# Two linear attentions run in steps beside an edge pass instead of in stages of their own

## The chip, the cores and the metric

The kernel runs on one core of a Trainium2 chip. The metric is the device time of one execution in microseconds. The kernel before took 8725.7 us (median of 3 runs, 8723.53 to 8730.71).

## The reference, cut to what matters

The program is a network of four layers over N = 3125 nodes with 256 features and 50000 edges sorted by target. Each layer takes the layer norm `xn` of `x` and adds two things to `x`: a graph convolution and an attention over all nodes. A feed-forward block follows. Only layers 1 and 3 matter here:

```python
# layer 1: attention without a softmax over pairs of nodes (4 heads of 32); k is exp'ed over the nodes
x = x + L1_gnn(xn, edge_index, edge_weight) + L1_mix(xn)     # both read xn alone
# L1_gnn, first of two convolutions
h = relu(x @ w1 + b1); agg = segment_sum(ew[:, None] * h[src], dst); h = agg @ w2 + b2
# layer 3: 4 heads of 64; k and v are layer-normed per head
k = _layer_norm(k, ln_k_g, ln_k_b); v = _layer_norm(v, ln_v_g, ln_v_b)
kv = einsum('bhsd,bhse->bhde', k, v) / S;  ga = einsum('bhsd,bhde->bhse', q, kv);  ga @ wo.T + bo
# L3_gnn: three graph convolutions with 1/sqrt(degree) on both sides
h = tanh(conv(x, W1, b1)); h = tanh(conv(h, W2, b2)); out = conv(h, W3, b3)
```

Both linear attentions compute a small matrix from all nodes first (k times v) and multiply every node's q by it afterwards. Neither needs anything of the graph convolution, nor the other way round.

## The kernel before, in words

All engines run one program each, written out by hand in order (`tensor_program`, `scalar_program`, `vector_program`, `gpsimd_program`, `sync_program`). An engine executes its instructions in that order. The stages are cut by `rest`: every engine drains, raises a semaphore and waits until all five have. Nodes lie in 25 tiles of 125 (`T`, `P`); `CH` are 7 chunks of 500 or 375 nodes. SBUF is one tensor, `arena`, cut by hand with `at(offset, ...)`. PSUM is 8 banks given out in turn by `Banks.take`, which also returns the key of the bank's holder before, so that the taker waits until that one was read. `put`, `land` and `of` are semaphores with a key for each value.

An edge pass (`pass_pool`, `pass_pe`, `pass_dve`) sums messages over sorted edges in KC = 416 steps of 128 edges. In step k POOL gathers 128 rows from a table in device memory (L1828), into a ring of `RING` = 6 buffers; it waits until the matmul of step k - 6 is done. DVE builds a one-hot matrix (L1861, with edge weights L1863), into a ring of 4, two steps ahead. PE multiplies the one-hot matrix by the rows (L1843), which the trace records as two matmuls with a weight load each. DVE adds the bank to the target tile (L1881), with a register for the tile's offset. Layer 1 has two such passes (`c1a`, `c1b`, rows of 256), layer 3 has three (`d3a` with 256, `d3c` with 512, `d3e` with 256), and layers 0 and 2 have one each, with attention weights per head: there DVE also multiplies the gathered rows in place (L1871).

The order around the change, before:

- Layer 1: the layer norm `n1`; `rest`; the attention as a stage (`l1_mix_*`, L632 to L749); `rest`; `l1_gnn_*`: SP loads 4 weights, 2 biases and 10 vectors (L2295, L2297, L134), PE waits for all of them and makes the table's rows (L297, L300), DVE and ACT add the bias and apply relu (L2342, L2343, L2356), SP writes the table in 5 DMAs (L2291), and the pass `c1a` begins.
- Layer 3: the norm `n3`; `rest`; the attention (`l3_mix_*`, L574 to L619, with `heads_*` and `queries_*`); `rest`; `l3_gnn_*`: SP loads, DVE scales the rows by the degree (L2537), SP writes the table, and the pass `d3a` begins.

In the attention of layer 3, k and v of a unit of 5 tiles are copied out of PSUM, centred per head, squared, summed and scaled (DVE L359 to L381; ACT L409, L414), then PE sums k times v over all tiles (L441), then for each chunk come q (L459), q times kv (L469), and the output product (L596), which DVE adds to X (L305). The functions that the change touches:

## Time and profile before

| | |
|---|---|
| median of 3 runs | 8725.7 us |
| profiled execution | 8726.65 us, span 8724.9 us |
| PE busy | 6441.2 us, 74% |
| DVE busy | 4647.5 us, 53% |
| POOL busy | 3782.1 us, 43% |
| ACT busy | 1029.3 us, 12% |
| mean granted TensorE clock | 0.736 of 2.4 GHz |

The shares are means over some twenty stages with different limits. The change concerns the two attention stages (77.68 us and 198.31 us) and the two passes behind them (529.7 us and 529.4 us), so those stretches have to be read one by one.

### The profile page before, as it was taken

The page shows a single profiled execution, that of the slowest core. Times are in us where ns is not written, and L with a number is a line of the kernel's source. Part 1 is how long each engine was busy: PE and PEld are TensorE (multiplying, and loading weights), DVE is VectorE, ACT ScalarE, POOL GpSimd, SP SyncE. Part 2 cuts the span into 40 slices and gives each one's busy share as a digit, 9 for nine tenths or more (in the row PEclk, how much of TensorE's full clock was granted, in tenths as well). Part 3 has the DMA queues.
Part 4 walks back from the last instruction along what each step waited for, and adds up shares of the span by engine and source line. Part 5 has one row for each costly group of instructions (what it writes and reads, how often), then busy time and mean ns, then how long its engine had stood idle before and what let it go on. Part 6 is the DMA issues. An engine that isn't in the chain of part 4 may idle for free. (4 is left out here: it accounts for less than half of the span.)

```text
span 8724.9 us, 74385 instructions
## 1 busy us (share of the span) xinstructions
PE 6441.2 (74%) x22206; PEld 3621.3 (42%) x22206; DVE 4647.5 (53%) x11112; ACT 1029.3 (12%) x2395; POOL 3782.1 (43%) x3733
## 2 busy tenths in 40 slices
PE   5756878838688677666769777496788888885786
PEld 4443433326433333355434423264333223433675
DVE  7574467772345455542454577866443586455211
ACT  2211001112100100111220011111001000000121
POOL 1874037705267467334000067300674575673222
PEclk9987556659865666679875576687566999565898
DMA  1101223326233233246001133200332565332554
GB/s 50 41 18 38 94 71 106 105 58 182 73 100 105 62 104 105 56 136 159 8 32 76 46 95 108 58 18 6 111 105 63 163 207 163 102 105 63 166 160 130
DMA packets 335705, 796.30 MB, mean 91 GB/s; under 512 B 79773, under 2 KB 189364, under 8 KB 321146
## 3 DMA queue, kind: packets, MB, share of 16 engines
q0 software_dynamic: 202752, 490.56, 21.3%
q1 hardware_dynamic: 132563, 300.99, 10.2%
q8 instruction: 190, 3.11, 0.1%
q14 instruction: 200, 1.64, 0.1%
HBM read 714.20 MB, written 77.09 MB: 91 GB/s over the span
## 5 line engine op out<-in xcount | busy, mean ns | idle before, releaser
L1843 PE MATMUL bank<-arena 128*125 128x256 f32 (+3 forms) x5824 | 3059.9, 631 | 763.2 <-DMA arena<-TAB,arena 353.5
L1828 POOL DMA_INDIRECT arena<-TAB,arena x2080 | 1967.1, 946 | 1596.7 <-DMA TAB<-arena 957.2
L1843 PEld LDWEIGHTS bank<-arena 128*125 128x125 f32 x5824 | 1248.1, 265 | 2573.6 <-DVE arena L1861 862.9
L1881 DVE TENSOR_TENSOR arena<-bank,arena 125x256 f32 (+3 forms) x2912 | 1359.5, 467 | 1381.0 <-PE bank L1843 1238.2
L1828 POOL DMA_INDIRECT arena<-TABa,arena x832 | 808.3, 972 | 1629.6 <-SPq L138 1374.2
L1861 DVE TENSOR_SCALAR arena<-arena 128x125 f32<-128x125 f32 x2080 | 674.3, 325 | 51.0 <-DMA TAB<-arena 50.9
L1465 POOL DMA_INDIRECT REC<-arena x400 | 471.8, 1180 | 290.1 <-DVE arena L1683 168.4
L1107 PE MATMUL bank<-arena 128*128 128x256 f32 x2048 | 484.9, 393 | 139.0 <-DVE arena L1265 70.7
L1056 POOL DMA_INDIRECT SUM<-arena x192 | 307.7, 1603 | 625.2 <-DVE arena L1277 590.3
L1274 DVE TENSOR_TENSOR arena<-bank,arena 128x512 f32<-128x512 f32 x96 | 66.4, 692 | 925.2 <-PE bank L1121 925.2
L297 PE MATMUL bank<-arena 128*125 128x256 f32 (+2 forms) x1600 | 426.9, 424 | 163.1 <-issue 40.1
L2027 PE MATMUL bank<-arena 125*128 125x100 bf16 (+1 forms) x2496 | 462.8, 321 | 53.3 <-DVE arena L2077 53.0
L1107 PEld LDWEIGHTS bank<-arena 128*128 128x128 f32 x2048 | 393.9, 196 | 214.3 <-issue 159.0
L1121 PE MATMUL bank<-arena 128*128 128x256 f32 x2048 | 458.7, 379 | 0.0
L1041 POOL DMA_INDIRECT arena<-XNT,arena x192 | 210.9, 1098 | 571.3 <-DVE arena L1244 513.7
L297 PEld LDWEIGHTS bank<-arena 128*125 128x125 f32 x1600 | 304.0, 199 | 279.9 <-issue 156.3
L1121 PEld LDWEIGHTS bank<-arena 128*128 128x128 f32 x2048 | 388.0, 189 | 55.6
L262 PE MATMUL bank<-arena 125*128 125x125 f32 x450 | 96.4, 398 | 391.3 <-DVE arena L239 336.4
L1143 ACT ACTIVATE arena<-bank,arena 128x256 f32<-128x256 f32 x512 | 242.9, 474 | 1027.3 <-PE bank L1107 1027.3
L1871 DVE TENSOR_TENSOR arena<-arena 128x260 f32<-128x260 f32 (+1 forms) x832 | 352.7, 424 | 20.2 <-DMA arena<-TABa,arena 19.4
L2077 DVE TENSOR_SCALAR arena<-arena 125x2048 bf16<-125x2048 bf16 x156 | 107.6, 746 | 350.8 <-DMA arena<-STR 350.8
L1863 DVE TENSOR_SCALAR arena<-arena 128x125 f32<-128x125 f32 x832 | 289.5, 349 | 0.0
(459 smaller groups left out, 6016.7 us busy)
## 6 DMA issues: line engine op xcount, KB each, us to landing
arena<-L_ffn_pack SPq DMA_DIRECT2D x32, 2054.0 KB, 8.8
arena<-L_ffn_pack SPq DMA_DIRECT2D x64, 1026.0 KB, 5.7
arena<-TAB,arena POOLq DMA_INDIRECT x2080, 2.8
arena<-SLR SPq DMA_DIRECT2D x52, 500.0 KB
arena<-DLR SPq DMA_DIRECT2D x52, 500.0 KB
arena<-TABa,arena POOLq DMA_INDIRECT x832, 2.8
TAB<-arena SPq DMA_DIRECT2D x20, 625.0 KB
arena<-L_ffn_b SPq DMA_DIRECT2D x96, 128.0 KB, 5.5
```

Source lines behind the costliest of these rows:

```text
L297: ins = e.matmul(ps[0:P, 0:f], srcT[:, kk, t * P:(t + 1) * P], W[:, kk, f0:f0 + f], start=(kk == 0), stop=(kk == k - 1 and not odd))
L1056: e.indirect_dma_start(out=SUM[:, :], out_offset=bass.IndirectOffsetOnAxis(ap=m.ridi[:, 2 * k + j:2 * k + j + 1], axis=0), in_=m.Y[k % 2][ ...
L1107: ins = e.matmul(ps[:, 0:SLOTS], w1[:, kk, oo * 128:(oo + 1) * 128], m.XE[i][:, kk, :], start=(kk == 0), stop=(kk == 1))
L1121: ins = e.matmul(ps[:, j * D:(j + 1) * D], m.H[i][:, kk, j * 128:(j + 1) * 128], w2[:, kk, :], start=(kk == 0), stop=(kk == m.hp - 1))
L1465: e.indirect_dma_start(out=REC[:, :], out_offset=bass.IndirectOffsetOnAxis(ap=ADR[:, b:b + 1], axis=0), in_=VAL[:, b, :], in_offset=None). ...
L1828: e.indirect_dma_start(out=m.G[k % RING][:, 0:m.width], out_offset=None, in_=m.table[:, :], in_offset=bass.IndirectOffsetOnAxis(ap=eidx[:, ...
L1843: e.matmul(ps[0:P, 0:m.full], m.S[k % SRING], m.G[k % RING], start=True, stop=True).then_inc(*put("pass_p", m.g, "summed", k))
L1861: ins = e.tensor_scalar(m.S[k % SRING], iotaL, edl[:, k:k + 1], None, ALU.is_equal)
L1863: ins = e.tensor_scalar(m.S[k % SRING], iotaL, edl[:, k:k + 1], m.weight[:, k:k + 1], ALU.is_equal, ALU.mult)
L1871: e.tensor_tensor(v, v, bcast(m.factor[:, k, :], c, 2), ALU.mult).then_inc(*put("pass_v", m.g, "weighed", k))
L1881: e.tensor_tensor(o, banks.of(m.g, "added", k)[0:P, 0:m.full], o, ALU.add).then_inc(*put("pass_v", m.g, "added", k))
L2027: e.matmul(o, sl[:, k * 128:(k + 1) * 128], a.as3[s], start=(s == 0), stop=False)
```

## The change

The stages of the attentions of layers 1 and 3 are taken out, with one `rest` each, on all five engines. Their PE and DVE programs become generators that yield a step number before each piece of work, and `pass_pe` and `pass_dve` of `c1a` and `d3a` run every piece whose number is due before their own step k. ACT, which has nothing to do in these passes, gets its part as one block in front of its next work. During these two passes the pass uses banks 0 to 3 and the attention banks 4 to 7 (in layer 3 two of them for projections, two for the pair of sums).

```diff
+    def beside(steps):
+        due = [next(steps, None)] if steps else [None]
+        def upto(k):
+            while due[0] is not None and due[0] <= k:
+                due[0] = next(steps, None)
+        return upto
-    def pass_pe(e, m):
+    def pass_pe(e, m, steps=None):
+        upto = beside(steps)
         for k in range(KC):
-            ps, before = banks.take(m.g, "added", k)
+            upto(k)
+            ps, before = banks.take(m.g, "added", k, **(LOW if steps else {}))
...
         for k in range(KC + 1):
+            upto(k)
             onehot(k + 2)
...
     def l3_mix_dve(e):
+        def spread(u):
+            yield U3 * u + 24
+            e.wait_ge(*of(g, "squared", u))
+            e.tensor_reduce(s2, tv, AX, ALU.add)
...
+        def scale(u):
+            yield U3 * u + 29
+            e.wait_ge(*of(g, "std", u))
+            e.reciprocal(s3, s3)
+            yield U3 * u + 30
+            e.tensor_tensor(vv, vv, bcast(s3, 64, 2), ALU.mult)
+            yield U3 * u + 33
+            e.tensor_tensor(vv, vv, bcast(gg, 20), ALU.mult)
+            yield U3 * u + 36
+            e.tensor_tensor(vv, vv, bcast(bb, 20), ALU.add)
...
+    def l3_weights_dve(e):
+        for W in m3W[1:]:
+            v = W.rearrange("p k (h c) -> p (k h) c", c=64)
+            settle(e, e.tensor_reduce(m3mean, v, AX, ALU.add), "mix_v")
+            settle(e, e.tensor_scalar(m3mean, m3mean, 1.0 / 64, None, ALU.mult), "mix_v")
+            settle(e, e.tensor_tensor(v, v, bcast(m3mean, 64, 2), ALU.subtract), "mix_v", "m3", "centred")
+        e.tensor_tensor(X, X, bcast(m3bo, T), ALU.add)
...
     def l3_gnn_sp(e):
+        l3_mix_sp(e)
+        table_sp(e, "d3a", TAB, d3acc, lambda t: ("d3a", "u", t))
         vec_t(e, d3b1, inp["L3_gnn_b1"]).then_inc(*land("deg_w"))
...
-        for v, name in ((d3W1, "W1"), (d3W2, "W2"), (d3W3, "W3")):
-            e.dma_start(v, mat(inp["L3_gnn_" + name])).then_inc(*land("deg_w", "d3", "loads"))
-        table_sp(e, "d3a", TAB, d3acc, lambda t: ("d3a", "u", t))
+        e.dma_start(d3W1, mat(inp["L3_gnn_W1"])).then_inc(*land("deg_w", "d3", "loads"))
+        e.wait_ge(*of("m3", "mm", T - 1))
+        for v, name in ((d3W2, "W2"), (d3W3, "W3")):
+            e.dma_start(v, mat(inp["L3_gnn_" + name])).then_inc(*land("deg_l", "d3", "later"))
...
     def l1_gnn_sp(e):
-        for v, name in zip(c1w, ("c1_w1", "c1_w2", "c2_w1", "c2_w2")):
-            e.dma_start(v, mat(inp["L1_gnn_" + name])).then_inc(*land("conv_w"))
+        e.dma_start(c1w[0], mat(inp["L1_gnn_c1_w1"])).then_inc(*land("conv_f"))
+        e.dma_start(c1bias[0], vec_n("L1_gnn_c1_b1")).then_inc(*land("conv_f", "c1a", "weights"))
+        l1_mix_sp(e)
+        for v, name in zip(c1w[1:], ("c1_w2", "c2_w1", "c2_w2")):
+            e.dma_start(v, mat(inp["L1_gnn_" + name])).then_inc(*land("conv_w"))
...
-        l1_mix_pe(e)
-        r = rest(e, r + 1)
-        banks.clear()
```

In layer 1 the work is the same (all copies out of PSUM now lie on ACT; before every second one was DVE's), the maximum of k is taken chunk by chunk, and the bias is added to X in 5 pieces. In layer 3 the centring of k and v (L359, L361, L363) is gone, replaced by six small operations on the weights in front of the pass (`l3_weights_dve`), and all copies are ACT's. In layer 1, `c1a` waits for its first weight and bias alone.

On PE, at the queries of layer 3, the program before had (L459 is q, L469 is q times kv, L596 the output product, L1843 the pass):

```order
L459 MATMUL bank<-arena 128x500 x4
L469 MATMUL bank<-arena 128x500 x2
L596 MATMUL bank<-arena 125x256 x8
L459 MATMUL bank<-arena 128x375 x4
L469 MATMUL bank<-arena 128x375 x2
L596 MATMUL bank<-arena 125x256 x6
...
L1843 MATMUL bank<-arena 125x256 x416
L1843 MATMUL bank<-arena 125x512 x416
```

Now one chunk of queries stands like this (L1988 is the pass, L643 is q, L653 is q times kv, L664 the output product):

```order
L643 MATMUL bank<-arena 128x500 x2
L1988 MATMUL bank<-arena 125x256
L643 MATMUL bank<-arena 128x500 x2
L1988 MATMUL bank<-arena 125x256 x5
L653 MATMUL bank<-arena 128x500
L1988 MATMUL bank<-arena 125x256
L653 MATMUL bank<-arena 128x500
L1988 MATMUL bank<-arena 125x256 x5
L664 MATMUL bank<-arena 125x256 x2
L1988 MATMUL bank<-arena 125x256 x2
L664 MATMUL bank<-arena 125x256 x2
```

A chunk's work is spread over 19 steps of the pass, at most two matmuls at a place.

On DVE, in the same pass, the program before repeated three rows (L1861 the one-hot, L1881 the add):

```order
L2537 TENSOR_SCALAR arena<-arena 125x256 x25
L1861 TENSOR_SCALAR arena<-arena 128x125 x4
L1875 TENSOR_LOAD arena
L1881 ISA
L1881 TENSOR_TENSOR arena<-bank,arena 125x256
L1861 TENSOR_SCALAR arena<-arena 128x125
```

Now the scaling of a unit of k or v stands between them (L2008 the one-hot, L2028 the add, L732, L735 and L738 the attention):

```order
L732 RECIPROCAL arena<-arena 125x20
L2008 TENSOR_SCALAR arena<-arena 128x125
L2028 ISA
L2028 TENSOR_TENSOR arena<-bank,arena 125x256
L735 TENSOR_TENSOR arena<-arena 125x1280
L2008 TENSOR_SCALAR arena<-arena 128x125
L2028 ISA
L2028 TENSOR_TENSOR arena<-bank,arena 125x256
L2008 TENSOR_SCALAR arena<-arena 128x125
```

Three operations of 125x1280 and one reduction of that size stand in every 24 steps, each alone in front of a one-hot.

On SP, at the start of layer 3's convolution, the program before had (W are the three weight matrices):

```order
L579 DMA arena<-woT 128x2x256
L580 DMA arena<-L_mix_bo 125x256
L134 DMA arena<-L_gnn_b 128x4x1 x2
L2450 DMA arena<-L_gnn_b 125x256
L2452 DMA arena<-L_gnn_W 128x2x512
L2452 DMA arena<-L_gnn_W 128x4x512
L2452 DMA arena<-L_gnn_W 128x4x256
L2291 DMA TAB<-arena 125x5x256 x5
```

Now the attention's 9 loads (the last two are shown) stand right in front of the table:

```order
L609 DMA arena<-woT 128x2x256
L610 DMA arena<-L_mix_bo 125x256
L2440 DMA TAB<-arena 125x5x256 x5
L134 DMA arena<-L_gnn_b 128x4x1 x2
L2607 DMA arena<-L_gnn_b 125x256
L2608 DMA arena<-L_gnn_W 128x2x512
L2611 DMA arena<-L_gnn_W 128x4x512
L2611 DMA arena<-L_gnn_W 128x4x256
```

The convolution's own loads moved behind the table's five writes.

## Rows read from the trace of the kernel before

**Rows 1.** Windows: layer 1's attention, table, pass c1a; layer 3's likewise; passes d3c, a0.
```profile
core 0: us, PE busy (x) PEld busy (x) DVE busy (x) ACT busy (x) POOL busy (x), PEclk, DMA share, GB/s
2308.29:2385.97 77.68, 61.76 (x295) 41.42 (x295) 29.82 (x60) 19.14 (x44) 0.00 (x0) 0.95 0.03 9
2385.97:2439.76 53.79, 33.58 (x124) 22.40 (x124) 16.01 (x31) 4.61 (x12) 5.43 (x2) 0.80 0.28 84
2439.76:2969.50 529.74, 436.34 (x833) 190.87 (x833) 286.54 (x828) 0.00 (x0) 393.58 (x416) 0.60 0.38 103
5907.19:6105.50 198.31, 126.82 (x484) 92.59 (x484) 129.91 (x158) 30.50 (x58) 0.00 (x0) 0.80 0.03 7
6105.50:6145.50 40.00, 0.00 (x0) 0.00 (x0) 7.76 (x30) 0.00 (x0) 0.00 (x0) 0.53 0.41 136
6145.50:6674.90 529.40, 445.39 (x832) 195.32 (x832) 259.33 (x829) 0.00 (x0) 393.40 (x416) 0.58 0.38 104
6839.00:7375.50 536.50, 452.72 (x862) 132.42 (x863) 427.26 (x844) 3.52 (x6) 390.50 (x414) 0.98 0.69 203
1223.00:1805.00 582.00, 444.50 (x832) 183.43 (x832) 445.45 (x1348) 86.46 (x418) 406.57 (x416) 0.61 0.37 96
```

**Rows 2.** Timeline of pass d3a, first steps: start, us, engine, line, operation.
```profile
6145.50 0.96 POOL L1828 DMA_INDIRECT arena<-TAB,arena  x1 [579.64 <-DMA TAB<-arena]
6146.76 0.95 POOL L1828 DMA_INDIRECT arena<-TAB,arena  x1 [0.30 <-issue]
6148.38 11.93 PE L1843 MATMUL bank<-arena 128*125 128x256 f32 x19 [43.42 <-DMA arena<-TAB,arena]
6149.72 0.43 DVE L1881 TENSOR_TENSOR arena<-bank,arena 125x256 f32 x1 [4.07 <-PE bank L1843]
```

**Rows 3.** Timeline, last steps of d3a: one step's matmuls, last gather, last add.
```profile
6661.73 1.19 PE L1843 MATMUL bank<-arena 128*125 128x256 f32 x2 [0.49 <-DMA arena<-TAB,arena]
6665.06 0.94 POOL L1828 DMA_INDIRECT arena<-TAB,arena  x1 [0.93 <-PE bank L1843]
6674.44 0.42 DVE L1881 TENSOR_TENSOR arena<-bank,arena 125x256 f32 x1 [0.90 <-PE bank L1843]
```

**Rows 4.** Timeline of SP, DVE and PE at the starts of both attentions and convolutions.
```profile
2312.95 6.83 DVE L720 TENSOR_TENSOR arena<-arena 125x6400 f32<-125x6400 f32 x1 [5.28 <-DMA arena<-L_mix_b_out]
2385.97 1.92 SPq L2295 DMA_DIRECT2D arena<-L_gnn_c_w  x4
2386.03 5.63 DVE L2411 TENSOR_SCALAR arena<-arena 128x416 int32<-128x416 f32 x1
2397.10 3.75 PE L297 MATMUL bank<-arena 128*125 128x256 f32 x8 [11.67 <-DMA arena<-L_gnn_bn_b]
2406.13 25.68 SPq L2291 DMA_DIRECT2D TAB<-arena  x5
5910.99 0.58 SPq L580 DMA_DIRECT2D arena<-L_mix_bo  x1
5917.30 6.83 DVE L608 TENSOR_TENSOR arena<-arena 125x6400 f32<-125x6400 f32 x1 [10.73 <-DMA arena<-L_mix_bo]
6105.57 0.38 DVE L2535 TENSOR_SCALAR arena<-arena 128x416 int32<-128x416 f32 x1
6109.30 25.31 SPq L2291 DMA_DIRECT2D TAB<-arena  x5
```

**Rows 5.** Groups by form in 5907.19 to 6105.50: DVE work that stays, per operation.
```profile
L377 DVE TENSOR_TENSOR arena<-arena 125x1280 f32<-125x1280 f32 x10 | 14.9, 1493 | 0.3
L305 DVE TENSOR_TENSOR arena<-bank,arena 125x256 f32<-125x256 f32 x25 | 10.6, 424 | 13.4 <-PE bank L596 13.4
```

**Rows 6.** Timeline of POOL in pass a0, 1434 to 1446: the lengthened gathers.
```profile
1437.43 1.23 POOL L1828 DMA_INDIRECT arena<-TABa,arena  x1 [0.30 <-PE bank L1843]
1438.96 1.12 POOL L1828 DMA_INDIRECT arena<-TABa,arena  x1 [0.30 <-PE bank L1843]
```

More of the change, by code:

```diff
@@ L63, in restart @@
     def restart(self):
-        self.n, self.held = 0, [None] * 8
+        self.n, self.held = {}, [None] * 8
     def clear(self):
@@ L286, in norm_pe, with lin_n_pe @@
         turn_pe(e, g, XN, lambda t: (g, "tile", t))
-    def lin_n_pe(e, g, srcT, k, W, f, tiles, f0=0, bias=None, sem="lin_p"):
+    def lin_n_pe(e, g, srcT, k, W, f, tiles, f0=0, bias=None, sem="lin_p", lo=0, hi=8):
         for t in tiles:
-            ps, before = banks.take(g, "out", t)
+            ps, before = banks.take(g, "out", t, lo=lo, hi=hi)
             if before:
@@ L583, in l3_mix_pe @@
         g = "m3"
-        heads_pe(e, g)
-        for ci, (n0, w) in enumerate(CH):
-            i = ci % 2
-            queries_pe(e, g, ci, (g, "kvs", 1))
+        yield 0
+        e.wait_ge(*of(g, "centred"))
+        for u in range(len(UNITS) + 1):
+            if u < len(UNITS):
+                t0, k = UNITS[u]
+                for j in range(5):
+                    yield U3 * u + 4 * j
+                    lin_n_pe(e, g + "kv"[k], XT, 2, m3W[1 + k], D, (t0 + j,), sem="mix_p", **PROJ)
+            if u and u % 2 == 0:
+                if u == 2:
+                    pair = [banks.take(g, "kvs", k, **PAIR)[0] for k in range(2)]
+                for j in range(5):
+                    yield U3 * u + 18 + j
+                    t = 5 * (u // 2 - 1) + j
+                    if j == 0:
+                        e.wait_ge(*of(g, "headed", u - 1))
+                    for k in range(2):
+                        ins = e.matmul(pair[k][:, 0:128], m3kN[:, t, k * 128:(k + 1) * 128],
+                                       m3vN[:, t, k * 128:(k + 1) * 128], start=(t == 0), stop=(t == T - 1))
+                        if t == T - 1:
+                            ins.then_inc(*put("mix_p", g, "kvsum", k))
@@ new lines, in l3_mix_pe @@
+        for ci, (n0, w) in enumerate(CH):
+            c0 = U3 * len(UNITS) + 24 + 19 * ci
+            for oo in range(2):
+                yield c0 + oo
+                ps, before = banks.take(g, "q", ci, oo, **PROJ)
+                if before:
+                    e.wait_ge(*of(*before))
+                for kk in range(2):
+                    ins = e.matmul(ps[:, 0:w], m3W[0][:, kk, oo * 128:(oo + 1) * 128], XT[:, kk, n0:n0 + w],
+                                   start=(kk == 0), stop=(kk == 1))
+                ins.then_inc(*put("mix_p", g, "qmm", ci, oo))
+            for k in range(2):
+                yield c0 + 6 + k
+                e.wait_ge(*of(g, "kvs", k))
+                e.wait_ge(*of(g, "q", ci, k))
+                ps, before = banks.take(g, "r", ci, k, **PAIR)
+                if before:
+                    e.wait_ge(*of(*before))
+                e.matmul(ps[:, 0:w], m3kvs[:, k, :], m3qc[ci % 2][:, k, 0:w], start=True, stop=True).then_inc(
+                    *put("mix_p", g, "rmm", ci, k))
@@ L638, in l1_mix_pe @@
         g = "m1"
-        e.wait_ge(*of(g, "loads"))
         for ci, (n0, w) in enumerate(CH):
-            ps, before = banks.take(g, "kT", ci)
+            yield 8 * ci
+            if ci == 0:
+                e.wait_ge(*of(g, "loads"))
+            ps, before = banks.take(g, "kT", ci, **HIGH)
             if before:
@@ L668, in l1_mix_pe @@
             ins.then_inc(*put("mix_p", g, "qmm", ci))
-            ps, before = banks.take(g, "o", ci)
+            yield c0 + 5
+            ps, before = banks.take(g, "o", ci, **HIGH)
             if before:
@@ L1851, in pass_act, with pass_dve @@
                 *put("pass_s", m.g, "extra", k))
-    def pass_dve(e, m):
+    def pass_dve(e, m, steps=None):
+        upto = beside(steps)
         offs = []
@@ L2308, in l1_gnn_pool, with conv_pe @@
             pass_pool(e, c1pass[g], (g, "table"))
-    def conv_pe(e, g, src, wa, wb, bias, ready=None):
-        e.wait_ge(*of("c1", "loads"))
+    def conv_pe(e, g, src, wa, wb, bias, ready=None, steps=None):
+        e.wait_ge(*of(*(("c1", "loads") if ready else (g, "weights"))))
         if ready:
@@ L2336, in conv_pe, with conv_dve @@
                 ins.then_inc(*put("conv_p", g, "secondmm", ci, oo))
-    def conv_dve(e, g, ba):
-        e.wait_ge(*of("c1", "loads"))
+    def conv_dve(e, g, ba, steps=None):
+        e.wait_ge(*of(*(("c1a", "weights") if steps else ("c1", "loads"))))
         for t in range(0, T, 2):
@@ L2344, in conv_dve @@
         e.wait_ge(*of(g, "zero"))
-        pass_dve(e, c1pass[g])
+        pass_dve(e, c1pass[g], steps)
+        e.wait_ge(*of("c1", "loads"))
         for ci, (n0, w) in enumerate(CH):
```

242 lines of the change are left out of this document (149 added, 93 removed).

## The prediction, made before the changed kernel ran

> **What bounds the kernel now.** I read the windows of the four stretches that the change touches, then the timeline inside the passes, then their ends. The windows [rows 1] say where the two attentions stand: 77.68 us in layer 1 and 198.31 us in layer 3, in which POOL does nothing, PE is busy for 61.76 and 126.82 us and DVE for 29.82 and 129.91 us. Behind each comes a stretch that makes the table (53.79 and 40.00 us) and then a pass of 529.7 and 529.4 us. In the passes PE looks fullest (436.34 and 445.39 us), but the time is POOL's. The first gather of d3a starts at 6145.50, the next 1.26 us later [rows 2], and the last of 416 at 6665.06 [rows 3], so the mean distance is 519.56 / 415 = 1.252 us: 0.95 us of gather and 0.30 us between two. PE needs two matmuls a step, 1.19 us from the first's start to the second's end [rows 3], and they are pipelined. What shows the room is the distance from a gather to the add of the same step: 6149.72 - 6145.50 = 4.2 us [rows 2]. The gather ring has 6 buffers, that is 6 x 1.25 = 7.5 us until POOL would wait. So PE and DVE together may come 3.3 us late before POOL loses anything, and whatever they are late by beyond that is lost for good, since POOL can't catch up. DVE is busy for 259.33 of 529.4 us [rows 1]. The pass d3c shows more: its matmuls have 512 columns, twice as many, PE is busy for 452.72 us, and the pass still takes 536.5 us. The granted clock there is 0.98, in d3a it is 0.58 (of the two levels, mostly the lower, 1.2 GHz).
>
> **Layer 1, what goes.** The attention's stage, from its first load to the next stage's first, is 77.7 us [rows 1]. Then c1a waits for 2 loads instead of 16. Before, PE starts 2397.10 - 2385.97 = 11.1 us after the stage's start [rows 4]. For the short wait the nearest row is the attention's own, where three loads were issued from 2308.29 on and the first work on them starts at 2312.95 [rows 1, 4]: 4.7 us. That gives 6.4 us, if SP isn't late with the table: the first table write follows PE's start by 2406.13 - 2397.10 = 9.0 us, so it can go at 13.7 us, and SP's 19 loads in front of it take about 19 x 0.48 = 9.1 us (four took 1.92 [rows 4]). Ends: 0 (PE's start hidden by DVE, which is held for 5.63 us, or by SP) and 7. I take 6.4.
>
> **Layer 3, what goes.** 198.3 us of stage [rows 1]. SP has 9 loads before the table instead of 6: they took from 5907.19 to 5910.99 + 0.58 = 5911.57, so 4.4 us, against 6109.30 - 6105.50 = 3.8 us [rows 1, 4]: +0.6 us. The attention's loads land at 5917.30, 10.1 us after the stage's start; then DVE does the six operations on the weights and the bias (6.83 us [rows 4]). None of the six is larger than an operation of 1280 elements (1.49 us [rows 5]), so all is done by 10.1 + 9 + 6.8 = 26 us, and the first gather needs 40.0 us for the table's sake [rows 1]. Cost nothing, with 14 us of cover.
>
> **What comes into the passes: PE.** By busy time it doesn't fit at today's clocks: 445.39 + 126.82 = 572 us in a pass of 529.4. At the lower level throughout, with the attention's busy time scaled from its clock of 0.80 to 0.5, it is 126.82 x 1.6 = 203 us, and 445 + 203 - 529 = 119 us too much; in c1a 61.76 x 0.95 / 0.5 = 117 and 436 + 117 - 530 = 24 us. That is one end, 143 us. At the upper level d3c shows twice the columns of d3a in 452.72 us of busy time, so d3a's own work takes about 226 us (an estimate, half of it) and the attention's about 126.82 x 0.80 = 101 us: 327 of 529 us, which fits easily; the other end is 0. Which clock? Columns per step of 1.25 us, from the code: d3a has 512 and gets 0.58, d3c has 1024 and gets 0.98. The attention of layer 3 adds on average 305 (127,100 columns in 416 steps), that of layer 1 167 (69,500). And where the lower level makes PE late, PE is busy without a gap; the attention's stage with such stretches has 0.80. So I expect a clock near 0.85 in d3a, near 0.75 in c1a, with intervals at the lower level in which PE falls behind by some tenths of a microsecond per step, most of it inside the 3.3 us. The nearest row is d3c, which has just that: 536.5 us against 529.4, of which some is its longer add. I take 8 us for d3a and 3 us for c1a.
>
> **DVE and the waits in order.** What stays of layer 3's DVE work is 4 operations of about 1.49 us in each of 10 units, 10.6 us of adds [rows 5] and some 5 us of small ones: 75 us, so 334 of 529. Pass a0 goes at the gathers' rhythm with 445.45 us of DVE [rows 1]. Cost nothing. Every piece of the attention waits in PE's and DVE's order, with the pass behind it. Each needs a copy by ACT, which is idle in both passes (0.00 us [rows 1]), and the numbers in the code leave two steps or more, 2.5 us, except where the second q matmul takes the bank of a product that DVE adds just then; that is under 1 us, 6 times, and inside the 3.3 us. Cost nothing; it is gone if PE is late already.
>
> **POOL's gathers beside long DVE operations.** 30 products of 125x1280 in layer 3 and 5 additions in layer 1, both inputs in SBUF, now run while POOL gathers. Of such company the trace has pass a0, where DVE multiplies the gathered rows: POOL is busy for 406.57 us against 393.40 in d3a [rows 1], with single gathers of 1.23 and 1.12 us [rows 6]. 13.2 us over 416 products is 0.032 us each; by their length, 1.49 to 0.42, it is 0.11 us, 4 us for 35. The other end: each holds POOL for its whole length, 35 x 1.49 = 52 us. That engines can block each other so is seen at 2386.03, where a DVE operation takes 5.63 us beside POOL's memset and 0.38 us at 6105.57 without it [rows 4]. I take 10 us (8 and 2), nearer to a0, since the kind is the same.
> The Trainium skill (SBUF — State Buffer, Who interferes with whom) says that a DVE instruction with two SBUF inputs contends with a GpSimd instruction that reads SBUF and that the one that starts second blocks fully, but also that `tensor_tensor` was not seen to stall a DMA. By the first sentence the sum would be nearer to the 52 us, by the second nearer to 0; the lengthened gathers of a0 speak for a little of the first.
>
> **Transfers.** W1 and the vectors of layer 3 are loaded while the pass begins, W2 and W3 (1.5 MB) near step 400. Bounds 0 and 8 us (all of it delays the last gathers); I take 3, because gathers near the end have the 3.3 us too.
>
> **The sum.** -77.7 - 6.4 - 198.3 + 0.6 + 11 + 10 + 3 = -257.8 us. From the profiled execution's 8726.65 that is 8468.9; the median stands 0.95 lower, so 8468 us. All prices at zero give 8444.
>
> **Rivals.**
> A. Nothing is held up: clock and ring cover all. 8444 us. For it: 3.3 us of room and idle ACT. Against: d3c is 7 us longer than d3a.
> B. Each long DVE operation holds a gather for its length: 52 instead of 10 us, 8510 us. For it the 5.63 us row; against it a0.
> C. The clock stays at the lower level in the passes and PE becomes the bound: 143 instead of 11 us, 8600 us. For it: d3a has 0.58 although PE is busy for 84%. Against it: d3c's 0.98 at the same rhythm.
> D. Slower than before. The in-order pieces and the pass alternate instead of overlapping: a piece stands in front of the pass's matmul, waits for its partner on ACT or DVE, and the room of the ring is used up because PE is late all the time. There are 121 + 128 = 249 pieces on PE. A handshake from PE to DVE takes 6149.72 - 6148.38 = 1.34 us [rows 2], 249 x 1.34 = 334 us against 281.8 saved: 8778 us. It decides from 281.8 / 249 = 1.13 us lost per piece. Against it: the distances of two steps and more.
>
> **Chances.** Forecast 0.62 (8450 to 8495), A 0.14, B 0.13, C 0.08, D 0.03. The range 8440 to 8550 holds the forecast, A and B. About 0.2% (17 us) can be told from no change: faster 0.96, same 0.01, slower 0.03.
>
> **What would show it.** The stages' windows are gone; from the last norm's copy to the first gather it is 47 us in layer 1 and 41 in layer 3. Pass d3a lasts 530 to 555 us, c1a 530 to 540, with the gathers still 1.25 us apart in most steps. The granted clock in d3a is above 0.75 (at 0.6 and PE busy without gaps it is C). POOL's idle times before L1828's successor above 0.30 us name PE; the sum of gather durations stays below 405 us (at 430 it is B). If POOL's waits are spread evenly over all places where attention pieces stand, it is D. I'm wrong if d3a takes more than 580 us or less than 525.

## The result and the profile after

| | before | after |
|---|---|---|
| median | 8728.15 us (4 runs, 8723.53 to 8730.71) | 8452.14 us (4 runs, 8448.95 to 8453.7) |
| profiled execution, span | 8726.65, 8724.9 us | 8448.95, 8447.2 us |
| mean granted TensorE clock | 0.736 | 0.769 |

The ratio is 0.9684, 95% interval 0.9667 to 0.9701. The forecast was 8468 us, in a range from 8440 to 8550. On the page of the changed kernel PE is busy for less time (by the clock, as will be seen) and DVE too (k and v are centred through the weights). POOL is busy for 17 us more; 13 of these are the long gathers below:

```profile
span 8447.2 us, 74344 instructions
PE 6140.4 (73%) x22206; PEld 3549.8 (42%) x22206; DVE 4589.9 (54%) x11029; ACT 1058.6 (13%) x2465; POOL 3798.8 (45%) x3733
```

The windows of the changed kernel answer to [rows 1]. The attention stages are gone. The five rows are layer 1's stretch from its first load to its first gather, then c1a up to 1.2 us after its last gather, layer 3's stretch and d3a likewise, and d3c:

```profile
core 0: us, PE busy (x) PEld busy (x) DVE busy (x) ACT busy (x) POOL busy (x), PEclk, DMA share, GB/s
2303.94:2353.43 49.49, 37.15 (x128) 24.23 (x128) 16.06 (x31) 5.21 (x13) 5.43 (x1) 0.84 0.36 105
2353.43:2876.88 523.45, 374.31 (x1113) 208.58 (x1113) 306.38 (x861) 28.90 (x73) 396.25 (x416) 0.85 0.37 104
5823.06:5860.71 37.65, 2.04 (x4) 1.17 (x4) 17.68 (x37) 0.38 (x1) 0.00 (x0) 0.50 0.41 130
5860.71:6394.30 533.59, 391.60 (x1302) 240.05 (x1302) 325.80 (x908) 48.11 (x97) 404.04 (x416) 0.90 0.37 105
6562.47:7084.10 521.63, 442.16 (x822) 124.42 (x822) 419.92 (x824) 0.00 (x0) 393.54 (x416) 0.99 0.71 208
```

The row of d3a in [rows 1] goes on to the last add, this one does not. The same window of the kernel before has 822 matmuls:

```profile
6145.50:6666.27 520.77, 439.42 (x822) 192.85 (x822) 256.39 (x821) 0.00 (x0) 393.40 (x416) 0.58 0.37 104
```

So in d3a PE executes 1302 matmuls instead of 822 and is nevertheless busy for less time, 391.60 us against 439.42: the granted clock rose from 0.58 to 0.90. In c1a it rose from 0.60 to 0.85. I compare passes by the time from the first gather to the last, which no neighbour blurs:

| | before | after | difference |
|---|---|---|---|
| layer 1, attention and table stretch | 77.68 + 53.79 | 49.49 | -82.0 |
| c1a, first to last gather | 519.7 | 522.2 | +2.5 |
| layer 3, attention and table stretch | 198.31 + 40.00 | 37.65 | -200.7 |
| d3a, first to last gather | 519.6 | 532.4 | +12.8 |
| d3c, first to last gather | 523.4 | 520.3 | -3.0 |

They add up to -270.4 of -277.7 us. Of the other 7.3, 3.9 are there before the first edge pass begins, in work that the change doesn't touch; a later execution of the same changed kernel was 5.1 us later at c1a's first gather (e9: 2358.49 against 2353.43), so this is the scatter of single executions. Counted to the last add, as the forecast counts a pass, d3a is 542.3 us and c1a 532.3, inside its 530 to 555 and 530 to 540.

**Where the 12.8 us of d3a are.** Some rows of the timeline of POOL in d3a of the changed kernel, unit 0's three products being due at steps 30, 33 and 36 (gathers of 0.95 us between them are left out):

```profile
5899.55 0.95 POOL L1971 DMA_INDIRECT arena<-TAB,arena  x1 [0.30 <-PE bank L1988]
5900.80 1.42 POOL L1971 DMA_INDIRECT arena<-TAB,arena  x1 [0.30 <-PE bank L1988]
5902.52 0.95 POOL L1971 DMA_INDIRECT arena<-TAB,arena  x1 [0.31 <-issue]
5905.02 1.09 POOL L1971 DMA_INDIRECT arena<-TAB,arena  x1 [0.30 <-PE bank L1988]
5908.92 1.17 POOL L1971 DMA_INDIRECT arena<-TAB,arena  x1 [0.30 <-PE bank L1988]
...
6281.95 0.95 POOL L1971 DMA_INDIRECT arena<-TAB,arena  x1 [0.93 <-PE bank L1988]
6283.89 0.94 POOL L1971 DMA_INDIRECT arena<-TAB,arena  x1 [0.99 <-PE bank L1988]
```

and the products on DVE in the same microseconds:

```profile
5899.91 1.48 DVE L735 TENSOR_TENSOR arena<-arena 125x1280 f32<-125x1280 f32 x1
5903.80 1.50 DVE L738 TENSOR_TENSOR arena<-arena 125x1280 f32<-125x1280 f32 x1
5907.79 1.48 DVE L741 TENSOR_TENSOR arena<-arena 125x1280 f32<-125x1280 f32 x1
```

The idle time in front of a gather stays 0.30 us, but the gather itself takes 1.42, 1.09 and 1.17 instead of 0.95 us. I call this a hold. Its size can be worked out. The first product ends at 5901.39, 0.59 us after the gather at 5900.80 began, and the gather is 0.47 longer. The second ends 0.28 after the start of its gather (+0.14), the third 0.35 (+0.22). Over all 30 products of the pass, the gather that starts while the product runs is longer by what is left of the product less 0.13 us (0.12 to 0.14 in every case). A gather that began before the product, if only 0.03 us, is left alone (one of the 30 is 0.05 us longer). The ten reductions over 125x1280 (L723), which read one input and take just as long, lengthen none. The lone gathers with 0.93 and 0.99 us of idle time are the other kind: there PE was late. All 416 durations add up to 404.0 us against 393.4 before, +10.6 (10.0 by the rule); the remaining 2.2 are waits for PE, at three gathers. The third has another cause. The two weights that the convolution needs later, 1.5 MB, are loaded from 6368.46 on, PE then waits 4.03 us for gathered rows, and POOL after it for PE:

```profile
6368.46 0.92 SPq L2611 DMA_DIRECT2D arena<-L_gnn_W  x2
6376.02 4.20 PE L1988 MATMUL bank<-arena 128*125 128x256 f32 x10 [4.03 <-DMA arena<-TAB,arena]
6377.48 0.94 POOL L1971 DMA_INDIRECT arena<-TAB,arena  x1 [1.25 <-PE bank L1988]
```

The same stands in e9, e10 and e11, 8 to 9 us after these loads are issued: PE waits 4.1 to 4.3 us for rows, POOL 0.78 to 1.18 us for PE. The kernel before, which loads these weights before the pass, has no such wait there; a run with the loads elsewhere was not made. So of the 2.2 us, 0.9 belong to the transfers, as far as the traces tell, and 1.3 to PE.

### The profile page after: what moved, and what is told of

It reads as the page before. It is cut to its first block and busy times, and to the rows that moved or that the text cites. A ratio compares the mean times of both kernels' runs of the same rounds, so it can differ in the third digit from the quotient of the medians.

```text
span 8447.2 us, 74344 instructions
## 1 busy us (share of the span) xinstructions
PE 6140.4 (73%) x22206; PEld 3549.8 (42%) x22206; DVE 4589.9 (54%) x11029; ACT 1058.6 (13%) x2465; POOL 3798.8 (45%) x3733
## 5 line engine op out<-in xcount | busy, mean ns | idle before, releaser
L1988 PE MATMUL bank<-arena 128*125 128x256 f32 (+3 forms) x5824 | 2778.0, 579 | 868.6 <-DMA arena<-TAB,arena 424.0
L1988 PEld LDWEIGHTS bank<-arena 128*125 128x125 f32 x5824 | 1158.1, 244 | 2458.9 <-DVE arena L2008 726.9
L2028 DVE TENSOR_TENSOR arena<-bank,arena 125x256 f32 (+3 forms) x2912 | 1358.9, 467 | 1302.2 <-PE bank L1988 1100.0
L2008 DVE TENSOR_SCALAR arena<-arena 128x125 f32<-128x125 f32 x2080 | 682.0, 328 | 35.2 <-DMA TAB<-arena 35.1
L297 PEld LDWEIGHTS bank<-arena 128*125 128x125 f32 x1600 | 312.3, 202 | 255.5 <-issue 155.6
```

The costliest lines, as they stand in the source:

```text
L297: ins = e.matmul(ps[0:P, 0:f], srcT[:, kk, t * P:(t + 1) * P], W[:, kk, f0:f0 + f], start=(kk == 0), stop=(kk == k - 1 and not odd))
L1988: e.matmul(ps[0:P, 0:m.full], m.S[k % SRING], m.G[k % RING], start=True, stop=True).then_inc(*put("pass_p", m.g, "summed", k))
L2008: ins = e.tensor_scalar(m.S[k % SRING], iotaL, edl[:, k:k + 1], None, ALU.is_equal)
L2028: e.tensor_tensor(o, banks.of(m.g, "added", k)[0:P, 0:m.full], o, ALU.add).then_inc(*put("pass_v", m.g, "added", k))
```

## The experiments

The experiments ran on four chips, called 2 to 5 here. Which chip the result above comes from isn't on record; it is called chip 1 and may be chip 4. The chips are not alike. On three of them the kernel before takes 9537 to 9571 us, and every pass, untouched ones too, is some 70 us longer: after runs of undisturbed gathers POOL stands still, mostly for 1 to 3 us. The timeline of POOL in d3a of e5, which is the kernel before with a smaller ring:

```profile
7297.51 0.95 POOL L1829 DMA_INDIRECT arena<-TAB,arena  x1 [0.30 <-issue]
7301.32 0.94 POOL L1829 DMA_INDIRECT arena<-TAB,arena  x1 [2.87 <-PE bank L1844]
```

The durations of the gathers and the usual 1.25 us between them are the same there. So I compare passes within one chip only, and the sum of the gathers' durations, which shows the holds, everywhere (in c1b, which nothing here touches, it differs by up to 2.7 us between runs). The sums in the expectations were added up from rounded rows and lie up to 0.9 us above these. The table has the time from first to last gather and the sum of the durations, in us; on chips 2 and 3 all runs but e7, and on chip 2 the kernel before too, are single runs.

| | before, there | this | c1a | sum | d3a | sum |
|---|---|---|---|---|---|---|
| chip 1: before | 8728 | | 519.7 | 393.6 | 519.6 | 393.4 |
| after | 8728 | 8452 | 522.2 | 396.2 | 532.4 | 404.0 |
| chip 2: e5 (before, ring of 4) | 9539 | 9538 | 592.0 | 395.4 | 591.3 | 393.3 |
| e4 (after, ring of 4) | 9539 | 9260 | 598.4 | 398.5 | 607.7 | 405.9 |
| e1 (lumps) | 9539 | 9358 | 619.3 | 398.8 | 675.0 | 401.2 |
| e2 (reductions) | 9539 | 9259 | 592.1 | 398.6 | 599.8 | 395.2 |
| chip 3: e3 (one input) | 9571 | 9303 | 599.7 | 401.3 | 611.7 | 401.5 |
| e6 (PE twice) | 9571 | 9324 | 598.7 | 399.7 | 629.9 | 404.8 |
| e8 (layer 1 alone) | 9571 | 9482 | 600.6 | 399.1 | 593.9 | 395.3 |
| e7 (less two-input work) | 9571 | 9308 | 598.5 | 395.2 | 616.3 | 402.8 |
| chip 4: e9 (after again) | 8730 | 8455 | 522.9 | 396.9 | 532.6 | 406.3 |
| e10 (pieces) | 8730 | 8457 | 519.7 | 393.6 | 531.4 | 404.2 |
| e11 (e7 again) | 8730 | 8453 | 519.8 | 393.7 | 528.4 | 401.0 |
| chip 5: e12 (e2 again) | 9537 | 9262 | 592.7 | 398.6 | 599.3 | 393.8 |

### e8: layer 1's half alone

Layer 3's functions, its stage and its `rest` are those of before; only layer 1's attention stands beside c1a.

> Only layer 1's attention runs beside its pass; layer 3 is as in the kernel before. If the parts are independent, the gain is that of layer 1 in the traces: 82.0 us of stage and earlier start less 2.5 us in the pass, so 8646 to 8650 us.

Measured: 9482.15 us in a single run, 89 less than the median of 9 runs of the kernel before there. In the changed kernel itself the terms of layer 1 are -82.0 + 2.5 = -79.5. Where the other 9 us are can't be said, because the kernel before wasn't profiled on that chip. Layer 1's half works without the other, and d3a without its partner has no held gathers (395.3, the longest 1.00 us).

### e1: the attention in lumps instead of steps

```diff
         def upto(k):
+            if k < KC and k % 26:
+                return
             while due[0] is not None and due[0] <= k:
```

> The changed kernel, but in passes c1a and d3a the attention's pieces are served only at every 26th step (and after the pass), on PE and DVE alike: 16 lumps in each pass, the same work and the same waits. Theory (it is the fine spreading over the 3.3 us of room in the gather ring that makes the attention free): a lump of d3a is 126.82 / 16 = 8 us of PE work at the least and 198 / 16 = 12 us with the waits of the old stage, less 3.3 us of room, so d3a grows by 75 to 145 us (from first to last gather 532 to about 610 to 680) and c1a by 20 to 35. Rival (the work is simply absorbed by idle time of PE and DVE, wherever it stands): both passes as in the changed kernel, within 10 us.

Measured: d3a +84 us against the kernel before with a smaller ring (e5, the control on that chip; 675.0 against 591.3), c1a +27. The expectation was an increase over the changed kernel, which didn't run there. Against its nearest kin there, e2 and e4, d3a is 75 and 67 us longer, at the lower end of what I expected. The work and its waits are the same, they only come in 16 heaps. The timeline of POOL and of PE at one heap:

```profile
6605.93 1.58 POOL L1973 DMA_INDIRECT arena<-TAB,arena  x1 [0.31 <-issue]
6616.01 0.95 POOL L1973 DMA_INDIRECT arena<-TAB,arena  x1 [8.50 <-PE bank L1990]
```

```profile
6608.43 1.47 PE L297 MATMUL bank<-arena 128*125 128x256 f32 x4 [2.83 <-ACT arena L679]
6609.80 3.77 PE L633 MATMUL bank<-arena 125*128 125x128 f32 x20
6613.41 1.90 PE L297 MATMUL bank<-arena 128*125 128x256 f32 x8
6615.15 2.16 PE L1990 MATMUL bank<-arena 128*125 128x256 f32 x8
```

PE stands in the attention's order until 6615.15 and waits 2.83 us for ACT inside it; POOL's ring of 6 is full, and POOL loses 8.5 us at once. This is rival D's mechanism in small. The step numbers avoid it.

### e4 and e5: a ring of 4 instead of 6

```diff
+            self.depth = 4 if g in ("c1a", "d3a") else RING
-            if k >= RING:
-                e.wait_ge(*of(m.g, "summed", k - RING))
+            if k >= m.depth:
+                e.wait_ge(*of(m.g, "summed", k - m.depth))
```

> The kernel before with 4 instead of 6 gather buffers in passes c1a and d3a alone: the control for the same edit in the changed kernel. Without attention pieces a step needs 4.2 of the 5.0 us, so both theories expect 520 to 530 us from first to last gather in either pass (519.7 and 519.6 with 6 buffers), the excess at the slow gathers of the last steps.

> The changed kernel with 4 instead of 6 gather buffers in passes c1a and d3a alone. From a gather to the add of its step it is 4.2 us, so 4 buffers of 1.25 us leave 0.8 us of room instead of 3.3. Theory (the ring's room is what hides the attention's bursts on PE): POOL loses part of each burst, 0.4 to 1 us at some 60 places in d3a and 40 in c1a: d3a 560 to 600 us from first to last gather instead of 532, c1a 535 to 560 instead of 522. Rival (PE is so fast at the upper clock that there are no bursts worth the name): within 5 us of the changed kernel.

Measured: the kernel before doesn't notice (9537.92 against 9539.06), and the changed kernel loses next to nothing either: d3a is 16.4 us longer than the control's, of which 12.6 are the durations of the gathers. So 3.8 us are left for everything that a smaller ring could expose, and e2, with a ring of 6, has more left (8.5 - 1.9 = 6.6), so this much is scatter on that chip. I had expected tens of microseconds; the rival was nearer. My picture of PE as often 2 to 3 us late, living on the ring's 3.3 us, is wrong. All this is from a chip with the stops, on which a gather comes every 1.42 us in the mean; a ring of 4 at 1.25 us was not run.

### e6: PE's part of layer 3's attention twice

```diff
-            for kk in range(k):
+            for kk in list(range(k)) * (2 if twice else 1):
```

and likewise for q, q times kv and the output product: each of these is computed twice, with the same result. Only the sums of k times v stay single.

> The changed kernel with layer 3's projections, queries and output products issued twice on PE (the same results; about 114,000 more columns in pass d3a, the pair sums not doubled). Theory (the granted clock rises with the work, so PE has room): d3a's clock 0.95 or more, the pass 10 to 40 us longer from first to last gather (532 before this edit), because bursts of four matmuls of 500 columns become eight, 3.4 us at the upper level, as much as the ring's room. Rival (PE was near its bound already): more than 90 us longer, as much as the added work's own time at the upper level.

Measured: 629.9 us of d3a. There was no unchanged copy on that chip. e3 and e7 there, brought to the same sum of durations, give 611.7 + 3.3 = 615.0 and 616.3 + 2.0 = 618.3, so +12 to +15 us for some 380 more matmuls. The windows of d3a in e6 and, behind it, in e7:

```profile
6492.57:7123.70 631.13, 482.44 (x1684) 324.37 (x1684) 326.62 (x908) 47.83 (x97) 404.84 (x416) 0.90 0.32 90
```

```profile
6486.84:7104.30 617.46, 426.22 (x1304) 273.44 (x1304) 311.87 (x898) 95.52 (x297) 402.77 (x416) 0.80 0.33 92
```

56 us more of busy PE cost a quarter of that. The clock is 0.90, not the 0.95 that I expected, against 0.80 in e7 and 0.83 in e3. PE isn't the bound; its room takes most of a second attention.

### e2 and e12: reductions in place of the products

```diff
-            e.tensor_tensor(vv, vv, bcast(s3, 64, 2), ALU.mult).then_inc(*put("heads_v"))
+            e.tensor_reduce(s2, vv, AX, ALU.add).then_inc(*put("heads_v"))
```

and so for all three; k and v are thus not scaled. Each reduction takes 1.48 us, as the product does, and reads one input.

> The changed kernel, but the 30 products and sums of 125x1280 of layer 3's attention in pass d3a, whose two inputs lie in SBUF, are reductions of the same 125x1280 with one input (k and v stay unscaled). Theory (a DVE operation with two inputs in SBUF holds back the gather that POOL starts meanwhile, one of one input doesn't): DVE stays as busy within 2 us, the gathers of d3a take 394 us in sum as in the kernel before instead of 404.7, and d3a from first to last gather 522 to 524 us instead of 532. Rival (the lengthening comes from DVE being busy, whatever it runs): 404 and 532 as in the changed kernel.

> e2 once more, for a chip on which the other passes aren't delayed (k and v of layer 3 are not normalized: each of the three products of a unit is replaced by a reduction over the same 125x1280, which reads one input). Theory (12.8 us of d3a's lengthening in the changed kernel are 10.5 of held gathers and 2.3 of gathers that PE's late work kept waiting): the durations of d3a's gathers add up to 394 to 396 us and its first to last gather takes 521 to 523 us against 532.4. Rival (part of the lengthening is something else, which e2's 599.8 us against 591.3 of the pass before on the second chip would be): the durations as before, but first to last gather 526 to 529 us.

Measured: the durations of d3a add up to 395.2 and 393.8 us. In e12 a gather starts during a reduction and isn't longer:

```profile
6513.02 0.95 POOL L1971 DMA_INDIRECT arena<-TAB,arena  x1 [0.30 <-PE bank L1988]
6514.27 0.95 POOL L1971 DMA_INDIRECT arena<-TAB,arena  x1 [0.30 <-PE bank L1988]
```

```profile
6513.83 1.48 DVE L735 TENSOR_REDUCE arena<-arena 125x20 f32<-125x1280 f32 x1
```

So the hold comes from the kind of operation, not from DVE being busy. What e12 was to settle beyond that it didn't: it came onto a chip with the stops again, and d3a there is 599.3 against 590.1 of d3c. The difference lies in stops (44 of over 1 us in d3a, 34 in d3c), and e2 has it too (599.8 against 591.3 of e5). Whether those 9 us would shrink to the 2.2 of the first chip stays open.

### e3: one-input products

```diff
-            e.tensor_tensor(vv, vv, bcast(gg, 20), ALU.mult).then_inc(*put("heads_v"))
+            e.tensor_scalar(vv, vv, 1.0, None, ALU.mult).then_inc(*put("heads_v"))
```

and so for all three; k and v are not scaled.

> The changed kernel, but the 30 products and sums of 125x1280 in pass d3a are multiplications by the constant 1.0 with one input in SBUF (tensor_scalar; k and v stay unscaled). The Trainium skill (SBUF — State Buffer, Who interferes with whom) says that such an operation can run in a mode that takes both ports and then contends with GpSimd. By that rule gathers are lengthened as with two inputs or more, by about the rest of an operation of 0.7 us: 10 to 20 us over the 30. If only the second input counts, the gathers take 394 us in sum as in the kernel before.

Measured: a sum of 401.5, between the products (404.0 to 406.3) and the reductions (393.8 to 395.2). The operation takes 0.83 to 0.89 us in the mean instead of 1.48 for the same elements, and it holds gathers all the same. Of 14 that began during one, 13 are longer by its remainder less 0.13 us, and here gathers already under way are drawn out too, by 0.03 to 0.35 us. Two gathers of e3, one of either kind:

```profile
6536.56 0.99 POOL L1971 DMA_INDIRECT arena<-TAB,arena  x1 [0.31 <-PE bank L1988]
6537.85 1.16 POOL L1971 DMA_INDIRECT arena<-TAB,arena  x1 [0.30 <-PE bank L1988]
```

Two inputs are then not the only condition. The one-input form runs at nearly twice the rate of the reduction (0.83 against 1.48 us); whether that is what sets them apart was not tried.

### e7 and e11: less two-input work in the passes

In layer 3 ACT multiplies by 1/std (20 instructions per unit), so DVE has two products instead of three. In layer 1 the bias is added before the pass begins, and the table is written ahead of the later loads.

```diff
+                ins = e.activation(vv[:, i, :], vv[:, i, :], ACT.Copy, scale=s3[:, i:i + 1])
-        for t0 in range(0, T, 5):
-            e.tensor_tensor(X[:, t0:t0 + 5, :], X[:, t0:t0 + 5, :], bcast(m1bo, 5), ALU.add).then_inc(
+            e.tensor_tensor(X, X, bcast(m1bo, T), ALU.add).then_inc(*put("mix_v", "m1", "biased"))
+        table_sp(e, "c1a", TAB, c1h, lambda t: ("c1a", "relu", t))
```

> The changed kernel with three edits against what is still lost: layer 1's bias is added to X before the pass, while DVE waits for the table (5 held gathers gone, 2.3 us), layer 1's 14 later loads are issued behind the table (the table's first write 3.1 us earlier), and the product by 1/std of layer 3's units is made by ACT in 20 pieces instead of by DVE (10 of the 30 holding operations gone, those that hold 0.4 to 0.9 us each: 5.7 us). Theory (two-input DVE operations hold gathers): 11 us less than the changed kernel, 8441 us. Rival (the hold isn't tied to these operations): 3 us less, from the loads alone.

> e7 once more, now beside the changed kernel itself. By the gather durations of its first run (c1a 395.8, d3a 403.1) it should be 3 + 2 us faster than the changed kernel for the holds, and up to 4 us for layer 1's table, whose write no longer stands behind the later loads on SyncE: 5 to 9 us in all. Rival: 0 to 3 us, if the table's write is no earlier, because VectorE's addition of the bias (2.4 us or more) now stands before the pass.

Measured: c1a's holds are gone in both (395.2, 393.7). In d3a taking away a third of the products took away 5.3 us in e11 (401.0 against 406.3), near the 5.7 that e7's expectation has, but less in e7 (402.8; e6 with all its products has 404.8 there). The 8441 us expected of e7 can't be compared, since it ran on chip 3 and the changed kernel didn't. The timeline of e11, POOL and then DVE:

```profile
5916.31 1.49 POOL L1971 DMA_INDIRECT arena<-TAB,arena  x1 [0.30 <-issue]
5920.60 1.09 POOL L1971 DMA_INDIRECT arena<-TAB,arena  x1 [0.30 <-PE bank L1988]
```

```profile
5915.50 1.48 DVE L744 TENSOR_TENSOR arena<-arena 125x1280 f32<-125x1280 f32 x1
5919.39 1.48 DVE L747 TENSOR_TENSOR arena<-arena 125x1280 f32<-125x1280 f32 x1
```

What a product costs is decided by where in the gathers' rhythm it begins. The first of a unit meets the gathers at any phase and still has 0.27 to 0.95 us to go when a gather starts, in one case 1.36 us, which gave +1.23. The later ones begin in step with PE and DVE's adds, and nine of ten have 0.27 us to go, which is +0.14. Removing one product therefore makes the next one the first. In the time, e11 is 8452.60 us (8448.69 to 8453.89) against 8455.26 (8450.77 to 8458.94) of the changed kernel beside it: 2.7 us, and the two ranges overlap. That is the rival's number, not the theory's 5 to 9. Of the 7.4 us that the two passes gained, 0.9 went in layer 1: from the first load to the first gather it is 50.1 instead of 49.2 us. The table's first write is hardly earlier (16.1 instead of 16.5 us after the first load), because it waited for the table's rows from PE and not for the loads. The first gather waits for the table to land, and after its last write was issued that took 8.35 us (8.32 in e10) instead of 6.97; in both the later loads are issued right behind that write, which may be the reason. The bias (6.82 us, below) now stands before the pass, as the rival has it, but it ends at 2357.01, and DVE's first one-hots at 2358.03, before the first gather at 2358.96.

```profile
2350.19 6.82 DVE L2498 TENSOR_TENSOR arena<-arena 125x6400 f32<-125x6400 f32 x1
```

### e9 and e10: the changed kernel again, and the products in pieces

```diff
-            e.tensor_tensor(vv, vv, bcast(bb, 20), ALU.add).then_inc(*put("heads_v", g, "headed", u))
+                    w = vv[:, 4 * j:4 * j + 4, :]
+                    e.tensor_tensor(w, w, other, op).then_inc(*put("heads_v", *key))
```

> The changed kernel itself, as the measure for the two beside it on the same chip. Expected against the kernel before as it was on the first chip: ratio 0.967 to 0.973 (the lower gain if this chip delays every gather as the second one did, since each delay is added to both). The durations of the 416 gathers of c1a add up to 397 to 399 us, those of d3a to 404 to 406 us.

> The changed kernel with layer 1's bias added before the pass and its later loads behind the table (as in e7), and with each of layer 3's three products per half of a unit cut from one instruction of 125x1280 into five of 125x256, two in a step of the pass over steps 24u+30 to 24u+37 of unit u. Theory (a gather is held only for the rest of the VectorE instruction that it meets, as the 0.42-us ones of a0's lengthened gathers there by 0.18 to 0.28 us at most): 15 short instructions a unit hold for less in all than 3 long ones: the durations of d3a's gathers add up to 399 us or less (405 in the changed kernel), those of c1a to 395 to 396, d3a is 5 to 8 us shorter than in the changed kernel, and the whole is 10 to 14 us faster than the changed kernel on this chip. Rival (what holds is the total time in which VectorE reads two inputs from SBUF, however it is cut, and the fixed cost of an instruction makes that longer, 15 x 0.36 = 5.4 us a unit against 4.5): sum of d3a's gathers 405 to 409 us, d3a as long as in the changed kernel or up to 5 us longer, and the whole 1 to 7 us faster, from layer 1 alone.

Measured: e9 repeats the result (ratio 0.9683, 0.967 to 0.9696). In e10 the sum of d3a is 404.2 (406.3 in e9) and the whole 8456.53 us (8455.26 in e9), so cutting gains nothing that can be told. POOL and then DVE of e10:

```profile
5905.30 1.20 POOL L1968 DMA_INDIRECT arena<-TAB,arena  x1 [0.30 <-PE bank L1985]
5906.80 1.19 POOL L1968 DMA_INDIRECT arena<-TAB,arena  x1 [0.30 <-issue]
5908.29 1.19 POOL L1968 DMA_INDIRECT arena<-TAB,arena  x1 [0.30 <-issue]
```

```profile
5904.92 0.75 DVE L744 TENSOR_TENSOR arena<-arena 125x256 f32<-125x256 f32 x2
5906.42 0.75 DVE L744 TENSOR_TENSOR arena<-arena 125x256 f32<-125x256 f32 x2
5907.92 0.75 DVE L744 TENSOR_TENSOR arena<-arena 125x256 f32<-125x256 f32 x2
```

Each of these pairs has 0.37 us to go when a gather starts and holds it for 0.24 us; the gathers then come every 1.50 us, and so does the next pair. 55 gathers of d3a are longer by 0.03 us or more instead of 35. The rule of the remainder holds here too, for the pair as a whole. My theory drew the wrong conclusion from it: the pieces lock into the rhythm of what they disturb. The rival's sum (405 to 409, counted from rounded rows; 405.0 counted so) is what was measured, though not its gain of 1 to 7 us.

## Why the prediction was right, and where its terms were off

- **Layer 1's stage**, -77.7: as forecast, an exact row.
- **c1a's earlier start**, forecast -6.4, measured 53.79 - 49.49 = -4.3. Both handovers in the term were a little later: PE starts 5.9 us after the first load instead of 4.7, and the table's first write follows PE by 10.9 us instead of 9.0. The landing behind the last write took 1.0 us less than before (6.97 against 7.95). SP's loads, which took 13.3 and not 9.1 us, were not the cause: e11 has them behind the table and writes only 0.4 us earlier. The write itself was as long as before (both tables' writes are below, then comes layer 3).

```profile
2309.85 3.75 PE L297 MATMUL bank<-arena 128*125 128x256 f32 x8 [6.50 <-DMA arena<-L_gnn_c_b]
```

```profile
2320.77 25.69 SPq L2440 DMA_DIRECT2D TAB<-arena  x5
5827.73 21.41 SPq L2440 DMA_DIRECT2D TAB<-arena  x5
```

- **Layer 3's stage**, -198.3 + 0.6: measured -200.7. The DVE work on the weights is covered, as forecast. The extra 3 us are the table: its five transfers are issued in 21.41 us instead of 25.31 [rows 4]. I hadn't thought of it and no experiment was made on it.
- **PE in the passes**, forecast 11, measured 1.3 in d3a and about 0 in c1a. The step that failed is the one from d3c's 536.5 us to the clock's cost: from first to last gather d3c took 523.4, only 3.8 more than d3a; the rest of its 7 us lies behind the last gather. The 3.8 are waits for PE, but the longest of them, 2.28 us at 6998.88, began with PE waiting for gathered rows:

```profile
6995.28 4.94 PE L1843 MATMUL bank<-arena 128*125 128x512 f32 x7 [2.33 <-DMA arena<-TAB,arena]
6998.88 0.94 POOL L1828 DMA_INDIRECT arena<-TAB,arena  x1 [2.28 <-PE bank L1843]
```

  e4 says how little room the pass needs, e6 how much it has. The two gathers in d3a that PE's own work delayed, at 6281.95 and 6283.89, follow a place that the forecast had priced at nothing: PE waits 0.95 us for DVE's add at 6279.30, because the second q matmul takes that bank. The clock was forecast near 0.85 in d3a and 0.75 in c1a, and came to 0.90 and 0.85.
- **POOL held by DVE**, forecast 10, measured 10.6 in d3a and 2.7 in c1a, together 13.3. The mechanism is the one forecast, shown by e2, e12 and e11's c1a. The way to its size was not, and that 10 is near 13 is luck. I took a0's 13.2 us for a hold of 0.032 us at each of 416 products, scaled it to 0.11 us and then took 10 us. But 6.9 of the 13.2 us are one gather, the pass's first:

```profile
1223.30 7.87 POOL L1828 DMA_INDIRECT arena<-TABa,arena  x1 [454.14 <-SPq L138]
1231.47 0.96 POOL L1828 DMA_INDIRECT arena<-TABa,arena  x1 [0.30 <-issue]
```

  By the rule found here a0's own products hold for 3.8 us in all. The right calculation is the remainder at the next gather's start less 0.13 us, 0.33 us each in d3a and 0.46 in c1a. With products at random phases of the 1.25 us it would be, as an estimate, about 1.35 x 1.35 / (2 x 1.25) = 0.73 us each, 25 us for 35 (1.35 is the product's length less 0.13); most of them begin in step with PE and DVE's adds, where less is left. Rival B (whole length each, 52 us) falls by the same rows, rival A by +12.8.

  The Trainium skill (SBUF — State Buffer, Who interferes with whom) has DVE and GpSimd share a port pair, with the second to start blocked until the first has finished. The remainder rule is that behaviour in this case's numbers, for POOL as the second. The other direction isn't seen here: all 30 products start during a gather and take 1.48 to 1.50 us, as in the stage before, where POOL did nothing (1.49 [rows 5]). The Trainium skill also has it there that `tensor_reduce` never contends on this chip, which e2 and e12 bear out (395.2, 393.8), and that `tensor_scalar` can, in its two-port mode. e3 contends (401.5); that it ran in that mode isn't shown. The Trainium skill's remark that `tensor_tensor` was not seen to stall a DMA doesn't hold for indirect ones: here 30 of 30 do, and the measurement decides.
- **Transfers**, forecast 3, measured 0.9: the wait at 6377.48 above, behind the loads of W2 and W3. The end of the pass doesn't notice them: last gather to last add is 9.45 us (6393.09 to 6402.54), against 9.4 before [rows 3].
- **d3c**, forecast 0, measured -3.0. There are fewer waits for PE, none above 1 us; why is not explained. In the changed kernel its clock was 0.99.

The terms that were too dear (PE 9.9, transfers 2.1, layer 3's table 3.0), the 7.3 us outside them and 3.0 of d3c make 25.3 us. The two that were too cheap (hold 3.3, c1a's start 2.1) make 5.4. The difference, 19.9 us, lies between a sum of -257.8 and the measured -277.7. The median stands 3.2 us above the profiled execution this time, so 8468 met 8452. The forecast was right in the mechanism and in the large terms, the two stages; the small ones were off by 2 to 10 us each, in both directions, and 10 us of the difference (outside the terms, and d3c) come from places that it didn't price.

Rival C falls by the clock rows (0.90 in d3a, 0.85 in c1a). Its price was too low besides: it scaled the attention's work to the lower level and not the passes' own, which from 0.58 and 0.60 to 0.5 would give, as an estimate, about 300 us instead of 143. D falls by e1 on one side and d3a's 2.2 us on the other: the added waits for PE are not spread over all 128 places but stand at three gathers.

## What to carry to other kernels

A stage that uses PE, DVE and ACT fits beside a pass whose bound is POOL's gather rhythm, if its pieces are spread so that no in-order engine is away from the pass for longer than the ring covers; in lumps the same work cost d3a some 70 us more than in steps (675.0 against 599.8 and 607.7 on that chip). Don't add up busy time at the old clock: look what the granted clock was in a stretch with that much work. Price every DVE operation beside a stream of gathers by what is left of it when the next gather starts: the reductions tried here were free, the elementwise operations from SBUF were not, and cutting them up locked them to the gathers. And look where large loads fall: the two issued near this pass's end made PE wait 4 us for gathered rows, and the ring hid all but 0.9 us of it.

## What the runs showed of the hardware that was not expected

- An indirect gather that starts while DVE runs a `tensor_tensor` from SBUF is longer by the remainder of that instruction less 0.13 us (30 of 30 in the changed kernel's d3a, 5 of 5 in c1a, all 20 in e11's d3a). One that started before the instruction, if only by 0.03 us, is not. A `tensor_scalar` of 125x1280 does it too, a `tensor_reduce` of the same size doesn't.
- The clock rose with the work so far that PE's busy time in d3a fell by 48 us with 58% more matmuls. On chip 3 the clock of d3a was 0.57 with 822 matmuls (e8), 0.83 and 0.80 with 1304 (e3, e7) and 0.90 with 1684 (e6).
- After the loads of W2 and W3, issued in 0.92 us, the DMA engines moved 345 GB/s between 6370 and 6375, and PE waited 4.0 us for the next gathered rows; e9, e10 and e11 have the same.
- The same kernel took 8728 to 8730 us in two measurements (perhaps on one chip) and 9537 to 9571 us on three other chips, with POOL's gathers interrupted by stops of mostly 1 to 3 us there, in every pass alike. The gain there is of about the same size: 9571.18 to 9307.51 for e7, 9539.06 to 9259.95 for e4. The cause of the stops was not looked for.
